# Cross-attention and ternary FFN kernel: first slot reordered around the variance, ternary column sums taken from ScalarE's passes, masks over fewer columns

## What is computed

```python
def bit_linear(x, w):      # w scaled by its mean |w|, rounded, clipped to -1, 0, 1
    scale = 127.0 / clip(max(abs(x), axis=-1), 1e-5)
    xq = clip(round(x * scale), -128, 127) / scale
    return xq @ weight_quant(w).T

q, k, v = ln(x) @ Wq.T + bq, ctx @ Wk.T + bk, ctx @ Wv.T + bv
sm = where(triu(ones((L, S)), k=1), -inf, q @ k.T / sqrt(32))
x = x + (softmax(sm) @ v) @ Wo.T + bo
h = bit_linear(ln(x), w1)                     # 512 -> 2048
h = silu(depthwise_conv1d(h, conv_w, conv_b)) # 3 taps along the sequence
x = x + bit_linear(h, w2)                     # 2048 -> 512
```

## Time and profile before

| | |
|---|---|
| median of 3 runs | 1546.28 us (1545.43 to 1548.14) |
| time of the profiled execution | 1545.68 us |
| its span, first to last instruction | 1543.9 us |
| busy share: TensorE / VectorE / ScalarE / GpSimd | 94% / 84% / 77% / 67% |
| mean granted TensorE clock | 0.967 of full |
| chain that ended last, by engine | TensorE 69%, VectorE 17%, ScalarE 9% |

### The profile page before, as it was taken

The page is one execution under the profiler, slowest core; times in us unless marked ns, Lnnn a source line. Parts: engine busy times, 40 slices in busy tenths (PEclk is TensorE's granted clock), DMA queues, the critical chain, the costliest instruction groups (busy, mean ns, idle before and its releaser), DMA issues.

```text
span 1543.9 us, 24821 instructions
## 1 busy us (share of the span) xinstructions
PE 1457.1 (94%) x9097; PEld 895.4 (58%) x9097; DVE 1296.0 (84%) x2014; ACT 1182.8 (77%) x2156; POOL 1036.6 (67%) x838
## 2 busy tenths in 40 slices
PE   9998797999999999999999999999999999998866
PEld 5475564747565665657565655657575656655322
DVE  7786697898879889898879898898979898878897
ACT  3565788979788887979787888879687878887652
POOL 4010375768686886968675977968676869778552
PEclk8998899999999999999999999999999999998987
DMA  8551002021310303021310303031212102020000
GB/s 254 152 183 41 29 8 69 7 57 46 62 64 7 97 7 97 8 70 39 75 42 15 90 7 97 8 101 21 68 37 45 60 9 68 8 70 1 31 28 29
DMA packets 80344, 85.22 MB, mean 55 GB/s; under 512 B 29983, under 2 KB 55839, under 8 KB 79709
## 3 DMA queue, kind: packets, MB, share of 16 engines
q1 hardware_dynamic: 80221, 83.62, 20.0%
HBM read 38.74 MB, written 19.42 MB: 38 GB/s over the span
## 4 chain that ended last, share of the span: by engine, by line
PE 69%; DVE 17%; ACT 9%; issue 3%; POOL 2%; DMA 0%; DVEq 0%; ACTq 0%; SPq 0%
PE ps L860 13%; PE ps L678 12%; PE ps L958 11%; DVE negm L1748 10%; PE ps L866 10%; PE ps L1042 9%; ACT hqb L1164 4%; ACT pexp L1243 3%; PE ps L829 3%; DVE h L1664 2%; PE ps L948 2%; PE ps L926 1%; PE ps L1012 1%; PE ps L1026 1%; PE ps L835 1%
## 5 line engine op out<-in xcount | busy, mean ns | idle before, releaser
L643 POOL TENSOR_TENSOR h<-h,gall 128x512 f32<-128x512 f32 x235 | 349.3, 1486 | 18.4
L653 POOL TENSOR_TENSOR h<-h,r 128x512 f32<-128x512 f32 x240 | 306.9, 1325 | 59.2 <-ACT r L1164 59.2
L641 POOL TENSOR_TENSOR gall<-gall,cw 128x512 f32<-128x512 f32 x235 | 257.4, 1095 | 109.6 <-DVE h L1664 109.6
L1664 DVE SCALAR_TENSOR_TENSOR h<-gall,cw,h 128x512 f32<-128x512 f32 x256 | 259.2, 1015 | 49.0 <-ACT h L1262 48.8
L860 PEld LDWEIGHTS ps<-va,pexp 128*128 128x128 f32 x2048 | 262.1, 194 | 29.0 <-issue 11.2
L1589 DVE SCALAR_TENSOR_TENSOR gall<-ps,bias,srow 128x512 f32<-128x512 f32 x256 | 191.1, 747 | 96.2 <-POOL h L643 59.2
L866 PE MATMUL ps<-xqT,w1T 128*128 128x512 f16 x1024 | 258.3, 382 | 7.8 <-DVE gall L1589 7.4
L860 PE MATMUL ps<-va,pexp 128*128 128x33 f32 x2048 | 260.1, 272 | 0.0
L1042 PE MATMUL ps<-w2T,hqb 128*128 128x512 fp8e4 x960 | 240.2, 379 | 0.0
L1262 ACT ACTIVATE h<-gall,cb,cw 128x512 f32<-128x512 f32 x256 | 222.2, 868 | 8.5
L1243 ACT ACTIVATE pexp<-ps 128x512 f32<-128x512 f32 x320 | 179.6, 588 | 58.0 <-PE ps L829 28.3
(11 more groups left out here) (221 smaller groups left out, 2319.3 us busy)
## 6 DMA issues: line engine op xcount, KB each, us to landing
qs<-hl SPq DMA_DIRECT2D x192, 128.0 KB, 2.6
xr<-in_x SPq DMA_DIRECT2D x16, 1024.0 KB, 5.6
out<-xr SPq DMA_DIRECT2D x64, 256.0 KB
h<-in_L_ffn_w SPq DMA_DIRECT2D x8, 1024.0 KB, 5.6
srow<-in_L_xattn_bo SPq DMA_DIRECT2D x15, 256.0 KB, 3.1
kst<-kh_scratch SPq DMA_DIRECT2D x32, 38.5 KB
xr<-in_ctx SPq DMA_DIRECT2D x1, 1024.0 KB
h<-in_L_xattn_Wk SPq DMA_DIRECT2D x1, 1024.0 KB, 8.2
```

Source lines behind the costliest of these rows:

```text
L641: gp.tensor_tensor(right, right, cw[:, c, 2:3].to_broadcast([P, TB]), ALU.mult).then_inc(c2m_ok, 1)
L643: gp.tensor_tensor(hc(c), hc(c), right, ALU.add).then_inc(c2p_ok, 1)
L653: gp.tensor_tensor(hc(c), hc(c), r2[:], ALU.mult).then_inc(u_ok, 1)
L1664: ve.scalar_tensor_tensor(out=hc(c), in0=g[:, c % 4, 1:TB + 1], scalar=cw[:, c, 1:2], in1=hc(c), op0=ALU.mult, op1=ALU.add).then_inc(c1_ok, 1)
```

## The change

It has five parts.
1. In slot 0 VectorE takes the maxima 0 to 3 ahead of `norm2`, and 4 to 7 between `norm2` and `quantise` (all eight stood between them before).
2. In slot 0 ScalarE makes the four `w2_half` passes right behind the squares, ahead of the quantised rows (they stood behind these).
3. The `w1_half` and `w2_half` passes also accumulate their row sums (into `bias1` and the new `wrow`). `w1_colsums` is gone; VectorE multiplies `bias1` by -1536 in place. `turn_o` of slot 0 waits for `w_out` in place of `w_bias`.
4. The 16 `w2_colsum` matmuls are replaced by four f32 matmuls of 128 columns that spread `wrow`, behind `query_scores` 0 of slot 1.
5. The mask of a score tile (L831) covers 128 columns in place of 154; the mask of query block i = 1 (L980) covers 2 x 26 columns in place of 2 x 154 (that of i = 0 stays whole).

```diff
-            def w1_colsums():
-                pe.wait_ge(w_out, CT)
-                for c in range(CT):
-                    for k in range(KT):
-                        r = mm(F[0][:, c:c + 1], w1T[:, k, c * P:(c + 1) * P], negh[:, 0:1], start=k == 0, stop=k == KT - 1)
-                r.then_inc(w_cs, 1)
...
-            def w2_colsum(c):
-                if c == 0:
-                    pe.wait_ge(x2_ok, at(1, TT, TT))
-                pe.wait_ge(w_out, CT + c + 1)
-                r = mm(F[1], onesh[:, 0:P], w2T[:, c, :], start=c == 0, stop=c == CT - 1)
-                if c == CT - 1:
-                    r.then_inc(w_cs, 1)
+            def w2_colsums():
+                pe.wait_ge(x2_ok, at(1, TT, TT))
+                pe.wait_ge(w_f16, CT + KT)
+                for i in range(KT):
+                    r = mm(F[1][:, i * P:(i + 1) * P], wrow[:, i:i + 1].to_broadcast([P, P]), identf[:], start=True, stop=True)
+                r.then_inc(w_cs, 1)
...
-                            r = mm(bank[:, 0:S], identh[:], maskk[:], start=False, stop=True, skip_group_check=True)
+                            r = mm(bank[:, 0:P], identh[:], maskk[:, 0:P], start=False, stop=True, skip_group_check=True)
...
-                            r = mm(bank, identh[:], maskq[:, i].unsqueeze(1).to_broadcast([P, 2, S]), start=False, stop=True)
+                            o = bank.rearrange("p (e s) -> p e s", s=S)[:, :, i * P:S]
+                            r = mm(o, identh[:], maskq[:, i, i * P:S].unsqueeze(1).to_broadcast([P, 2, S - i * P]),
+                                   start=False, stop=True, skip_group_check=True)
...
-                copy(w1tern[:, c, :], w1nat[:, c, :], bias=-ROUND).then_inc(w_f16, 1)
+                copy(w1tern[:, c, :], w1nat[:, c, :], bias=-ROUND, accum_out=bias1[:, c:c + 1]).then_inc(w_f16, 1)
...
-                copy(w2tern[:, i, :], w2nat[:, i, :], bias=-ROUND).then_inc(w_f16, 1)
+                copy(w2tern[:, i, :], w2nat[:, i, :], bias=-ROUND, accum_out=wrow[:, i:i + 1]).then_inc(w_f16, 1)
...
                     for i in range(TT):
                         square(i)
+                    if s == 0:
+                        for i in range(KT):
+                            w2_half(i)
...
-                    act.wait_ge(w_cs, 2)
+                    act.wait_ge(w_cs, 1)
...
-                dve.wait_ge(w_cs, 1)
-                ve.tensor_copy(bias1[:], F[0][:, 0:CT]).then_inc(w_bias, 1)
+                dve.wait_ge(w_f16, CT)
+                ve.tensor_scalar(bias1[:], bias1[:], -HALF, None, ALU.mult).then_inc(w_bias, 1)
...
+                if s == 0:
+                    for n in range(4):
+                        maximum(n // NG, n % NG)
                 if do_a:
                     norm2()
...
                 if s == 0:
-                    for n in range(8):
+                    for n in range(4, 8):
                         maximum(n // NG, n % NG)
                 if do_a:
                     quantise()
```

More of the change, by code:

```diff
@@ L95, in build @@
         bias1 = sb("bias1", [P, CT], F32)
+        wrow = sb("wrow", [P, KT], F32)
         bqc = sb("bqc", [P, NG], F32)
@@ L944, in turn_o @@
                         if k == 2 and s == 0:
-                            pe.wait_ge(w_bias, 1)
+                            pe.wait_ge(w_out, CT)
                             pe.wait_ge(w_scale, 4)
@@ L977, in query_scores @@
                         r = mm(bank, qhl[:, 0, k, i * P:(i + 1) * P], kB[:, k, half * PAIR:(half + 1) * PAIR],
-                               start=True, stop=not masked)
+                               start=True, stop=True)
                         if masked:
-                            r = mm(bank, identh[:], maskq[:, i].unsqueeze(1).to_broadcast([P, 2, S]), start=False, stop=True)
+                            o = bank.rearrange("p (e s) -> p e s", s=S)[:, :, i * P:S]
+                            r = mm(o, identh[:], maskq[:, i, i * P:S].unsqueeze(1).to_broadcast([P, 2, S - i * P]),
+                                   start=False, stop=True, skip_group_check=True)
                     r.then_inc(sq_ok, 1)
@@ L1060, in slot @@
                         w1_turn(2 * (c - 2) + 1)
-                    if s == 0 and c == 10:
-                        w1_colsums()
                     if s == NB and c in (8, 10, 12, 14):
@@ L1123, in slot @@
                         v_main(2, (n - 3,))
-                    if s == 1:
-                        w2_colsum(n)
+                    if s == 1 and n == 0:
+                        w2_colsums()
                     if do_a and do_m:
@@ L1437, in slot @@
                                              scale=qm1[:, 3, i:i + 1]).then_inc(xq_ok, 1)
-                if s == 0:
-                    for i in range(KT):
-                        w2_half(i)
                 if late_results(s):
@@ L1587, in dequant @@
                         dve.wait_ge(src, at(s, 1, 0))
+                        if s == 1:
+                            dve.wait_ge(w_bias, 1)
                     dve.wait_ge(h1_ok, at(s, CT, c + 1 - CT))
@@ L1811, in slot @@
                         w1_copy(2 * (c - 3) + 1)
-                    if s == 0 and c == 11:
+                    if s == 0 and c == 9:
                         w1_bias()
```

## The result

The changed kernel takes 1531.86 us (median of 4 executions, 1530.79 to 1533.41), the kernel before it 1547.21 us beside it (4 executions, 1545.43 to 1561.66): ratio 0.9881, 95% interval 0.9839 to 0.9922. The ratio here is that of the means, 1531.98 and 1550.38 us, and one execution at 1561.66 us weighs in it. The two profiled executions differ by 13.0 us (1545.68 and 1532.68 us; spans 1543.9 and 1530.9 us), the medians by 15.4. Most of what follows is about that difference.

What follows compares the result with a forecast made beforehand. TensorE bounds the kernel, and what counts is when it can begin `mm1_ahead`. Terms of -6.0, -1.6, +0.2, -0.9 and -1.9 make -10.2 us, with clock effects likeliest -12: 1534 us, range 1529.8 to 1539.0.

Steps and rivals of the forecast that it cites:

- The tail: End of slot 0: parts 1 and 2 start `mm1_ahead` earlier, -6.0 us; full clock there, -1.5 us more.
- the four accumulator reads: ScalarE, slot 0 tail: each w2 pass also reads the accumulator, 0.1 to 0.19 us each.
- the stall of the last two maxima: Slot 0 tail: `query_scores` 14 and 15 queue behind the first `turn_xq`, which waits for quantised rows; 0.6 us.
- w1 sums: Slot 0: 64 matmuls removed, -1.6 us; ScalarE's accumulator reads, +0.2; full clock from 115 us, -2.6 more.
- w2 sums: End of slot 1: ScalarE's wait for column sums goes, four f32 matmuls stand against it; net -0.9 us.
- The feared fall among the maxima of slot 1: Slot 1 without the 512-column matmuls: if the clock falls, its end pays about 1.5 us.
- Masks: Slots 3, 7, 11 and -1: shorter masks save VectorE's 0.15 us wait at each masked maximum, -1.9 us in all.
- The weight load that I kept as a floor: Masked query blocks: with 52 columns the streaming nearly goes, but the next weight load stays.
- The score mask: Score tiles: 26 of 154 columns saved 64 times, but `pv`'s weight loads hold TensorE; 0, at most -0.7 us.
- The sum: Whole kernel: -10.2 us without any clock change, -12 likeliest with some of the clock effects.
- -14.3: Whole kernel: total in us with full clock both in slot 0's tail and in the stretch from 115 us.
- The base: Start of the forecast: profiled execution of 1545.68 us gives 1533.7; median 0.6 us above it, so 1534.

Runs made afterwards that it cites:

- the filled pair: e13 and e12: the kernel before and the changed kernel, both with unread 512-column matmuls in slot 0's first steps; 1545.87 and 1530.48 us.
- e14: e13 with part 1 alone (maxima 0 to 3 ahead of the variance): 1545.07 us.
- e1: The whole changed kernel run again beside the kernel before: 1532.45 us, ratio 0.9889.
- e12: Changed kernel plus unread 512-column matmuls in the first steps of slot 0: 1530.48 us, ratio 0.9852 to the kernel before.
- e13: Kernel before plus the same unread 512-column matmuls as e12: 1545.87 us, ratio 0.9948 to the plain kernel before.
- e2: Kernel before with parts 1 and 2 alone (order of maxima and w2 passes): 1541.76 us, ratio 0.9936.
- e4: Kernel before with part 5 alone (masks): 1547.88 us, ratio 0.9984.
- e8: Changed kernel plus eight unread 512-column matmuls where the w1 column sums stood: 1534.1 us, ratio 0.9917 to the kernel before.
- e9: Kernel before with parts 3 and 4 alone (column sums), a repeat run: 1542.8 us, ratio 0.9953.
- e11: Changed kernel plus one or two unread 512-column matmuls behind each of slot 0's first 14 query scores: 1535.41 us, ratio 0.9892 to the kernel before.
- e5: The kernel before, unchanged, profiled once more: 1561.86 us.

## Why the forecast was too small

**The tail, -6.0 and -1.5 for the clock: right.** Measured -7.3 (28.89 to 21.58 us, and the same in the filled pair). By its own steps: w2 passes at once behind the squares; the four accumulator reads cost 0.10 us each (153.83 - 146.26 = 7.57 us for the four, against 165.31 - 158.13 = 7.18 without in e14), at the low end of 0.1 to 0.19; the stall of the last two maxima was 1.20 in place of 0.6 us; the clock came back at 161.1 us, just ahead of `mm1_ahead` (1.89 us in place of 2.47) and behind most of the spread.

**w1 sums, -1.6, +0.2, and -2.6 for the clock: right.** Between the two first traces the loop and the stretch behind it gave 0.83 + 1.92 = 2.75 us, less than the 4.0; but the changed kernel's fall at 86 us lasted 10.2 us there, against 6.8. Beside e1, whose fall is 6.8 us too, it is 2.36 + 1.92 = 4.3 us, and 4.3 again with that fall filled away on both sides (e12, e13). e2 and e4, which keep the column sums, need 36.1 + 30.3 us there, 7 more than the changed kernel's 32.95 + 26.42; their falls of 13.7 and 10.2 us are longer than the 6.8 and 6.8 of the first profile. What the 16 reads of the accumulator cost is not shown by itself.

**w2 sums, -0.9: right.** Slot 1 is 0.59 us shorter between the first traces, and 0.8 in the mean of the 9 traces with this edit (89.3 to 91.2) against the 9 that keep the w2 column sums (90.5 to 91.8), which overlap. The feared fall among the maxima of slot 1 came in five of the 9 traces with the edit (3.4 us in the changed kernel, 6.8 in e8, e9, e11 and e12). In the 9 others it begins there in none, but in three (e5, e13, e14) a fall of 3.4 us begins just ahead of the first query score, and these are the three at 91.8. With the edit slot 1 takes 89.3 to 89.7 us in the other four, 90.3 with the short fall and 91.2 with the long ones: the fall costs 0.6 to 2 us where it comes, about what the forecast put on it.

**Masks, -1.9: mis-sized, a quarter too small.** I let the gain of a masked maximum stop at VectorE's wait of 0.15 us. Measured is 0.95 - 0.74 = 0.21 us, since the masked maximum itself took 0.80 us and not the 0.72 of an unmasked one. On TensorE: two matmuls of 308 columns take 0.27 us, one of 308 and one of 52 take 0.16 (412.61 to 412.77), and saved twice per maximum that gives 0.22. The weight load that I kept as a floor does not show. Slots 2 to 14 take 1109.3 to 1110.0 us in the ten traces without this edit and 1106.8 to 1107.9 in the eight with it: 2.4 us, where 1.8 were forecast. Whether slot -1 gained too is not shown, as its end scatters (81.6 to 85.3 us) from start-up. The score mask gave nothing that can be seen, as forecast.

**The sum: the first step that failed.** "The likeliest is one to two of these three coming with a small loss: -12." The three are the two gains of full clock, -1.5 and -2.6 us, and the fall in slot 1. Both gains came: the second in full, as the w1 term above shows, the first nearly (spread and `mm1_ahead` take 1.30 + 1.89 = 3.19 us in place of 4.34). What the fall in slot 1 took back is already in the 0.6 us measured there. The prediction's own sum with both gains, -14.3, is what the runs show where the clock of the loop is alike on both sides: 14.3 us by the traces of e12 and e13, 14.2 between `before` and e1, whose falls at 88 us are both 6.8 us long. The 2.3 us between -14.3 and -12 were a discount on the clock that the runs did not bear out. That -14.3 fits so closely is in part luck: masks 0.6 and w1 sums 0.3 us more, tail 0.2 and slot 1 0.3 less, and 0.4 us given back at the start and in the last slots.

**The base: the second step that failed.** "Against the profiled execution (1545.68 us) that is 1533.7; the median lies 0.6 us above it, so I predict 1534." That took the clock of slot 0 as a property of the kernel. It is a draw: the fall at 85 to 88 us lasted 6.8 us in that trace, and in the twelve others without the start filler 6.8 to 14 us nine times and about 50 us three times (e5, e9, e11). The first profile was a lucky draw, as were the three times beside it: only 8 of the 99 executions are as fast as 1545.68 us, and their median is 4.2 us above it, while the changed kernel's first profile (1532.68 us) lies 0.2 us from its median in e1. So between the plain kernels the medians differ by 15.4 us in the first runs and 17.7 in e1, and the ratio, with its one long execution, says more still. The range had no term for this. That 1534 lies only 2.1 us from the measured 1531.86 is therefore luck: a base that was too fast and a sum that was too small made up for each other. What fixes how long a fall lasts in a given execution of one and the same program stays open, and also whether the change itself shortens it (one of its 10 plain executions, 1552.47 us, lies far out); that the times grow narrower without it is shown (e13 beside the plain kernel).

The trace of the changed kernel also loses 1.05 us in the last slots against that of before. That column goes from 168.50 to 170.58 us over all traces, and the kernel before alone has 168.95 and 170.04, so this is not shown to be the change's.

## What to carry to other kernels

When engine A waits for B's input, look at what independent work of A stands behind the waiting instruction, and move it into the hole: here that one move was 6 of 15 us, and the finer split around it 1.5, by the traces. Before adding terms to a profiled time, see how that execution lies among others of the same kernel and what its clock did, since a sum can be right and its base off by more than the terms. Thin matmuls cost more than their time when they bring the clock down; here removing them gave it back behind the loop, and wide ones whose results nobody reads kept it up at the start of slot 0.

## What the hardware showed that I had not expected

- TensorE can be busy for all of 48 us and be granted half its clock, 1.2 in place of 2.4 GHz (87.8 to 135.6 us in e5), in the same program that in another execution had it back after 6.8 us. The Trainium skill, "TensorE: Matmul & The Clock Gate", Part 1, has the throttled state as the default, which activity releases; the trace shows in addition that a busy TensorE is not enough: between 100 and 132 us its busy time is 2.00 of 2.00 us at 0.50.
- Adding work made the kernel before faster: with twelve matmuls of 512 columns more at the start of slot 0 its ratio is 0.9948 [0.992, 0.9976]. In the changed kernel they took the loop over c from 32.95 to 29.64 us.
- Behind 64 matmuls of one column (1.75 us) the stretch to the first query score took 30.59 us, and behind 8 of 512 columns (1.89 us) 26.39.
